# An attention and quantised-linear kernel: the tile work of two units done in every second unit

## The reference

```python
xn = _layernorm(x, axis=-1)
q = (xn @ Wq.T).reshape(n, s, HEADS, HEAD_DIM)              # k, v: 8 heads, each used twice
energy = jnp.einsum('nqhd,nkhd->nhqk', q, k) + _alibi_bias(s, s)
attn = jax.nn.softmax(energy / jnp.sqrt(jnp.float32(HEAD_DIM)), axis=-1)
out = jnp.einsum('nhqk,nkhd->nqhd', attn, v).reshape(n, s, HEADS * HEAD_DIM) @ Wo.T + bo

x_scale = jnp.maximum(jnp.max(jnp.abs(xn), -1, keepdims=True), 1e-6) / 127.0
x_q = jnp.clip(jnp.round(xn / x_scale), -128, 127).astype(jnp.int8)
lin = (x_q @ weight_q.T) * x_scale * weight_scale[None, :] + bias

x + out + lin
```

## Time and profile before

| | us |
|---|---|
| median of 3 runs | 1603.3 (1603.0 to 1604.26) |
| the profiled execution | 1604.17 |
| its span on the core | 1602.4 |
| TensorE busy | 1567.9, 98% |
| VectorE busy | 1429.5, 89% |
| ScalarE busy | 1220.8, 76% |
| GpSimd busy | 1066.9, 67% |

### The profile page before, as it was taken

The page is one execution under the profiler, slowest core; times in us unless marked ns, Lnnn a source line. Parts: engine busy times, 40 slices in busy tenths (PEclk is TensorE's granted clock), DMA queues, the critical chain, the costliest instruction groups (busy, mean ns, idle before and its releaser), DMA issues.

```text
span 1602.4 us, 53471 instructions
## 1 busy us (share of the span) xinstructions
PE 1567.9 (98%) x22012; PEld 785.0 (49%) x22012; DVE 1429.5 (89%) x1666; ACT 1220.8 (76%) x2394; POOL 1066.9 (67%) x1595
## 2 busy tenths in 40 slices
PE   5899999999999999999999999999999999999998
PEld 4344444545545545545545545545545545444443
DVE  6999999999999999999999999999999998999981
ACT  4477777777787787787787787787787787888875
POOL 5577787787777777777777777777777776333332
PEclk9999999999999999999999999999999999999999
DMA  8222222232232232223233223223223222111111
GB/s 195 71 69 59 72 75 62 77 79 79 81 79 80 82 78 80 82 75 83 81 77 81 82 73 85 82 75 83 81 73 85 79 67 62 52 52 50 45 46 54
DMA packets 182215, 121.03 MB, mean 76 GB/s; under 512 B 99988, under 2 KB 154644, under 8 KB 181972
## 3 DMA queue, kind: packets, MB, share of 16 engines
q1 hardware_dynamic: 181972, 117.62, 27.4%
HBM read 81.40 MB, written 35.63 MB: 73 GB/s over the span
## 4 chain that ended last, share of the span: by engine, by line
PE 83%; DVE 7%; SPq 4%; issue 3%; DMA 2%; POOL 1%; ACT 1%; DVEq 0%; POOLq 0%; ACTq 0%
PE ps_pv L1227 25%; PE ps_ring L1163 24%; PE ps_row L1163 24%; DVE row_max L885 4%; PE ps_ring L1259 3%; SPq L417 3%; PE ps_ring L1278 3%; DMA token_b<-token_dram 2%; PE ps_ring L1262 1%; PE ps_ring L1272 1%; DVE xn L812 1%; PE ps_row L1251 1%; DVE stats L802 1%; ACT probs L1048 1%; PE ps_ring L1178 0%
## 5 line engine op out<-in xcount | busy, mean ns | idle before, releaser
L885 DVE TENSOR_REDUCE row_max<-ps_row 128x1 f32<-128x1024 f32 x1024 | 1204.5, 1215 | 109.4 <-PE ps_row L1163 108.5
L1048 ACT ACTIVATE probs<-ps_ring 128x512 f32<-128x512 f32 x2048 | 1114.0, 600 | 216.1 <-PE ps_ring L1163 165.2
L1163 PE MATMUL ps_ring<-q,k 122*32 122x512 bf16 x8192 | 727.9, 379 | 1.7 <-ACT probs L1048 1.0
L1163 PE MATMUL ps_row<-k,q 120*32 120x512 bf16 x8192 | 635.7, 380 | 10.8 <-issue 4.9
L674 POOL TENSOR_TENSOR probs<-probs,near 128x256 f32<-128x256 f32 x512 | 380.8, 744 | 301.9 <-ACT probs L1048 255.9
L1227 PE MATMUL ps_pv<-probs,v_unit 128*32 128x512 f32 x4096 | 537.4, 593 | 5.5 <-POOL probs L674 5.5
L1163 PEld LDWEIGHTS ps_row<-k,q 120*32 120x32 bf16 x8192 | 240.4, 97 | 327.1 <-issue 159.5
L1163 PEld LDWEIGHTS ps_ring<-q,k 122*32 122x32 bf16 x8192 | 232.3, 95 | 318.4 <-issue 129.4
L1227 PEld LDWEIGHTS ps_pv<-probs,v_unit 128*32 128x32 f32 x4096 | 130.9, 110 | 81.6 <-POOL probs L674 10.9
L697 POOL TENSOR_TENSOR xt_step<-xt,token_b 128x256 f32<-128x256 f32 x53 | 45.8, 863 | 66.2 <-PE ps_ring L1163 46.0
L1259 PEld LDWEIGHTS ps_ring<-xn_t,wqk 128*128 128x128 f32 x636 | 78.7, 192 | 2.4
(11 more groups left out here) (85 smaller groups left out, 916.2 us busy)
## 6 DMA issues: line engine op xcount, KB each, us to landing
parts_dram<-parts SPq DMA_DIRECT2D x59, 288.0 KB, 3.3
token_b<-token_dram SPq DMA_DIRECT2D x53, 256.0 KB, 3.4
q<-parts_dram SPq DMA_DIRECT2D x128, 96.0 KB
q<-parts_dram SPq DMA_DIRECT2D x128, 64.0 KB
att_dram<-att_unit SPq DMA_DIRECT2D x126, 64.0 KB
att_t<-att_dram SPq DMA_DIRECT2D x56, 128.0 KB, 2.9
out<-out_tile SPq DMA_DIRECT2D x55, 128.0 KB, 2.9
xt<-x_t SPq DMA_DIRECT2D x53, 128.0 KB, 3.1
```

Source lines behind the costliest of these rows:

```text
L885: dve.tensor_reduce(row_max[:, par, e, qb:qb + 1], ps_row[qb % 2][:, :], AX_X, ALU.max, negate=True).then_inc(row_max_found, 1)
L1048: act.activation(probs[:, c % PBUFS, e, h * HALF:(h + 1) * HALF], ring_bank(u, c, e, h), ACT.Exp, scale=SCALE).then_inc(ring_freed, 1)
L1163: mm = pe.matmul(to[at, :], weights[:, at], moving, start=start, stop=stop)
```

## The change

Tiles are worked on in pairs. TensorE makes and projects two tiles in every odd unit and none in even ones (`made_unit`, `projected_unit`): in odd u, tiles u+9 and u+10 are made and tiles u-9 and u-8 projected, with `outputs` of both first and then `qkv_whole` of both, in four items of the ring. VectorE normalises two tiles and finds the statistics of two in odd units, at the same place of c=1, and none in even ones. GpSimd goes on turning one tile a unit; xt, xn_t and xq_t have four buffers (xt had four already), the scales eight. Of a pair, GpSimd splits the first tile at c=1 and the second at c=2 and c=3, weighs the first's linear result at c=4 and adds it at c=7, the second's at c=1 and c=2 of the next unit. Scaling, rounding and keeping a turned tile stand at c=4, 5 and 6. The first tiles' linear results are weighed at c=1 and added at c=4 of even units. Token factors are stored in pairs and loaded one a unit, ahead of `place_max` and no longer behind `load_set`. x is loaded two units earlier. At the start, quantised tiles are turned one step later. At the end, tile 55 is projected in unit 63 with tile 54, and the first part of the last sequence's projection goes over units 62 and 63, four products each.

```diff
-X_AHEAD = PREP_AHEAD + 3
+X_AHEAD = PREP_AHEAD + 5
+PAIR = 2
+TURNED = 4
-SCALES = 4
+SCALES = 8
+def made_unit(t):
+
+    return t - PREP_AHEAD + 1 + (t + 1) % PAIR
+
+
+def projected_unit(t):
+    return t + OUT_BEHIND - t % PAIR
 def flags_of(u):
 
+    pairs = u % PAIR == 1
-        made=0 < u and u - 1 + PREP_AHEAD < TILES,
-        normed=u + 1 + PREP_AHEAD < TILES,
-        stats=u + 2 + PREP_AHEAD < TILES,
+        made=[t for t in range(PREP_AHEAD, TILES) if made_unit(t) == u],
+        normed=[PREP_AHEAD + 1] * (u == 0) + [t for t in (u + PREP_AHEAD + 1, u + PREP_AHEAD + 2)
+                                             if pairs and t < TILES],
+        stats=([PREP_AHEAD + 2, PREP_AHEAD + 3] * (u == 0)
+               + [t for t in (u + PREP_AHEAD + 3, u + PREP_AHEAD + 4) if pairs and t < TILES]),
...
-        proj=u >= OUT_BEHIND,
+        proj=[t for t in range(TILES) if projected_unit(t) == u],
...
-        xn_t = sb("xn_t", [P, 2, EC, P])
-        xq_t = sb("xq_t", [P, 2, EC, P], BF16)
+        xn_t = sb("xn_t", [P, TURNED, EC, P])
+        xq_t = sb("xq_t", [P, TURNED, EC, P], BF16)
...
@@ sp: unit @@
-                if f["normed"]:
-                    store_token(u + 1 + PREP_AHEAD)
-                if f["made"]:
-                    store_parts(u - 1 + PREP_AHEAD, (u - 1 + PREP_AHEAD) % 2)
+                for t in f["normed"]:
+                    store_token(t)
+                for t in f["made"]:
+                    store_parts(t, t % 2)
...
+                if f["token"]:
+                    load_token(u + 1 + PREP_AHEAD)
                 if not f["last"]:
                     place_max(u + 1, (u + 1) % SETS)
...
-                if f["normed"]:
-                    load_token(u + 1 + PREP_AHEAD)
...
@@ gpsimd: unit @@
+                    if c == 1:
+                        for made in f["made"][:1]:
+                            split_high(made)
+                            split_middle(made)
+                    if c == 2:
+                        for made in f["made"][1:]:
+                            split_high(made)
...
+                    if c == 3:
+                        for made in f["made"][1:]:
+                            split_middle(made)
...
+                    if f["prev"] and c in (1, 2):
+                        for made in flags_of(u - 1)["made"][1:]:
+                            if c == 1:
+                                weigh_linear(made)
+                            else:
+                                add_weighted(made)
...
@@ vector: unit @@
-                    if c == 1 and f["normed"]:
-                        normalise(t + 1, (t + 1) % 2)
-                        find_largest(t + 1, (t + 1) % 2)
-                        find_scale(t + 1, (t + 1) % 2)
-                    if c == 1 and f["stats"]:
-                        wait(dve, x_loaded, 16 * (t + 2 - X_AHEAD + 1))
-                        find_stats(t + 2, t % 2)
+                    if c == 1:
+                        for t in f["normed"]:
+                            normalise(t, t % 2)
+                            find_largest(t, t % 2)
+                            find_scale(t, t % 2)
+                        for t in f["stats"]:
+                            wait(dve, x_loaded, 16 * (t - X_AHEAD + 1))
+                            find_stats(t, t % 2)
...
@@ tensor: unit @@
                     if c == 1:
-                        if f["made"] or f["proj"]:
-                            outputs(u, f)
-                        if f["made"]:
-                            qkv_whole(u)
+                        for t in f["proj"] or f["made"]:
+                            outputs(u, f, t % PAIR)
+                        for t in f["made"]:
+                            qkv_whole(u, t)
```

More of the change, by code:

```diff
@@ L109, in ring_places @@
             if c == 1:
-                items += [(u, "outputs")] * (f["made"] or f["proj"])
-                items += [(u, "qkv")] * f["made"]
+                items += [(u, "outputs", t % PAIR) for t in f["proj"] or f["made"]]
+                items += [(u, "qkv", t % PAIR) for t in f["made"]]
             if c == 5 and not f["last"]:
@@ L287, in build @@
         xt_loaded = [sem(f"xt_loaded{i}") for i in range(2)]
-        token_stored = sem("token_stored")
+        token_stored = [sem(f"token_stored{i}") for i in range(2)]
         token_loaded = [sem(f"token_loaded{i}") for i in range(2)]
@@ L340, in build @@
         CONSTS = 16 * 4
+        FIRST_BOTH = min(t for t in range(PREP_AHEAD, TILES) if flags_of(made_unit(t))["proj"])
         ALIBI = 16
@@ L354, in wait_lin_kept, with stored_tokens, finished @@
         def wait_lin_kept(eng, t):
-            u = t - PREP_AHEAD + 1
+            u = made_unit(t)
             if flags_of(u)["proj"]:
-                eng.wait_ge(lin_scaled, u - OUT_BEHIND + 1)
+                eng.wait_ge(lin_scaled, t - FIRST_BOTH + 1)
             else:
-                wait_freed(eng, u, "outputs")
+                wait_freed(eng, u, "outputs", t % PAIR)
+        def stored_tokens(t):
+            return 16 * ((t - PREP_AHEAD) // 2 + 1)
+        def finished(u):
+            return [t for t in range(TILES - BLOCKS)
+                    if u == min(projected_unit(t) + t % PAIR, UNITS - 1)]
         def run_units(unit):
@@ L750, in finish @@
             def finish(t):
-                wait_freed(pool, t + OUT_BEHIND, "outputs")
+                wait_freed(pool, projected_unit(t), "outputs", t % PAIR)
                 if t < PREP_AHEAD:
@@ L782, in unit @@
                         gather_v(u + 1, (u + 1) % 2)
-                    if c == 6 and f["stats"]:
-                        find_rstd(t + 2, t % 2)
+                    if c == 6:
+                        for later in f["factor"]:
+                            find_rstd(later, later % 2)
                     if c == 6 and f["turned"]:
                         keep_rounded(t)
-                    if c == 6 and u < PREP_AHEAD:
-                        add_first_linear(u)
-                    if c == 7 and f["proj"]:
-                        finish(u - OUT_BEHIND)
+                    if c == 7:
+                        for made in f["made"][:1]:
+                            add_weighted(made)
+                    if f["prev"] and c in (1, 2):
+                        for made in flags_of(u - 1)["made"][1:]:
+                            if c == 1:
+                                weigh_linear(made)
+                            else:
+                                add_weighted(made)
+                    if c == 1:
+                        for first in f["first_linear"]:
+                            weigh_first_linear(first)
+                    if c == 4:
+                        for first in f["first_linear"]:
+                            add_first_linear(first)
+                    if c == 7:
+                        for done in finished(u):
+                            finish(done)
             run_units(unit)
@@ L1252, in project_last, with qkv_whole @@
                           start=(c == 0 and i % 2 == 0), stop=False)
-            def qkv_whole(u):
-                t, bank = u + PREP_AHEAD - 1, take_bank(u, "qkv")
+            def qkv_whole(u, t):
+                bank = take_bank(u, "qkv", t % PAIR)
                 pe.wait_ge(xn_t_ready, t + 1)
```

196 lines of the change are left out of this document (93 added, 103 removed).

## The result

The changed kernel takes 1619.96 us (median of 4 runs, 1619.15 to 1620.67), against 1603.15 for the kernel before on the same chip (4 runs, 1601.17 to 1604.26): the ratio is 1.0106, with 1.0089 to 1.0124 as its 95% interval. It is slower by 16.8 us. 1626 was forecast, with 1608 to 1640 as the range. The profiled execution took 1620.67, its span 1618.9.

A forecast was written before the change was run, and what follows sets the result against it. TensorE was taken as the bound, with VectorE's side work just hidden (0.11 us in hand). Terms 0.9 + 0.6 - 0.6 + 20.8 + 3.1 - 2.5 + 0.4 = +22.7 on 1604.17 gave 1626 as median; range 1608 to 1640.

The forecast's parts named there:

- Odd units: Units carrying two tiles on TensorE: 2 x 2.88 + 0.21 = 5.97 of tile work, so 26.86 us a unit, no wait.
- 0.86 in hand: VectorE's slack at c=1 of odd units: 0.11 + 2.88 of cover - 2.13 of added tile work.
- Even units: Without tile work as cover, TensorE waits 0.85 to 1.37 us for VectorE at i=6; 1.3 taken, 22.19 a unit.
- Units 9 to 53: Middle of the kernel: 23 odd units and 22 even ones, 1106.0 against 1085.2 us, so +20.8.
- Units 1 to 8: Units that don't project: 192.8 against 193.4 us, so -0.6, with waits of 3.00 in unit 1 and 1.10 in odd ones.
- Start and unit 0: Start: last quantised tile turned a step later, +0.9; unit 0: one more tile's statistics at c=1, +0.6.
- Units 54 to 61, 62 and 63: End of the kernel: units that only project +3.1, unit 62 -2.5 with projections moved out, unit 63 +0.4.
- The earlier load takes that away: Token factors loaded ahead of the maxima: removes GpSimd's three-microsecond late start on the turned tile, gains nothing.
- TensorE alone as the bound: Rival: VectorE's wait in even units stays small, the change is faster, 1587 without any wait; chance 0.10.
- GpSimd always first: Rival: GpSimd's 0.74 us falls on the norm in nearly all even units, wait 1.6, 1635 us; chance 0.15.
- A wait on SP in odd units: Rival: second tile's parts late, maxima placed late, TensorE waits at even units' start; 1640 and more; chance 0.10.
- GpSimd clear of the norm: Rival: no GpSimd operation beside the norm, wait 0.85 in even units everywhere, 12.5 less, 1613 us; chance 0.10.

The follow-up runs named there:

- extra_odd6: Changed kernel with six more VectorE reductions of 256 values at c=1 of odd units 11 to 53, results unused: 1637.6 us, ratio 1.0219.
- linear_later: Changed kernel with GpSimd's second-tile weighing at c=2, its adding at c=3 and first tiles' weighing at c=3 in even units: 1615.37 us, ratio 1.0073.
- token_late: Changed kernel with the token factors loaded behind the set again, as in the kernel before: 1627.27 us, ratio 1.0148.
- before_token: Kernel before with only the token factors' load moved ahead of the maxima, as the change has it: 1597.33 us, ratio 0.9965.
- mid_sp: Changed kernel, even units: norm between reductions i=6 and i=7, turn back between i=8 and i=9, maxima ahead of attention on SP: 1584.46 us, ratio 0.9883.
- spread34: Changed kernel with the reciprocals and norm at c=3 and the turn back at c=4 of even units, SP's order unchanged: 1604.46 us, ratio 1.0018.
- before_mid: Kernel before, every unit: norm between reductions i=6 and i=7, turn back between i=8 and i=9, maxima ahead of attention on SP: 1599.12 us, ratio 0.9975.
- s45_sp: Changed kernel, even units: norm at c=4, turn back at c=5, maxima ahead of the attention's store and load on SP: 1594.76 us, ratio 0.9949.

## Why the prediction was right, and where its steps were not

**Odd units: right.** 26.86 was forecast and is what all 23 odd units from 9 to 53 show to 0.02. That the ring holds when a tile follows a tile is shown by the 0.45 at the change of tiles. "0.86 in hand" was half of what extra_odd6 shows, 1.68. The term that failed is the tile work of 2.13: it contained an xn of 0.82 that had GpSimd beside it, and without it is 1.72; 0.11 + 0.41 + 2.88 - 1.72 = 1.68. It cost the forecast nothing, since slack isn't time.

**Even units: right mechanism, size within its bounds.** "It waits 0.85", with 1.37 as the other end and 1.3 taken. Measured were 22.07 - 20.89 = 1.18 in the middle, and 0.97 without contention (linear_later). The 0.12 by which 0.85 is low is the turn back, which now follows the norm that it depends on: 0.46 from start to start (1437.10 to 1437.56 in unit 56), where xn, which doesn't, follows at 827.58 - 827.24 = 0.34. What the norm loses beside GpSimd is 0.21, between the forecast's 0 and 0.52; taking half was a choice between two readings, and it came out near. By the rule of the Trainium skill ("SBUF - State Buffer", the section on two separate sides: the first of the two keeps the shared port for its whole instruction) 1635 was given, with 0.74 more: GpSimd had in fact begun first, 0.38 earlier, and the norm did end 0.29 behind it, at 805.80 after 804.79 + 0.72 = 805.51. So the trace agrees with the rule, and the rival priced the whole operation where only what is left of it at the norm's start counts. Units 4, 6 and 8 show the rival nearly whole: there the weighing of a first tile began 0.06 before the norm, the norm took 0.95, and the units take 22.40, a wait of 1.51 where that rival had 1.6.

**Units 9 to 53**: +20.8 forecast, +18.1 measured, and 22 x (1.3 - 1.18) = 2.6 is the difference.

**Units 1 to 8: wrong size**, -0.6 against -3.4. Unit 1's wait was put at 3.00; the bracket shows 1.82, and by the period it is 25.13 - 20.89 - 2.11 = 2.13. The odd units' 1.10 is 25.25 - 20.89 - 4.01 = 0.35. Both used the 2.13 of tile work, which holds for a late load of the token factors: token_late, which has that, has -0.1 in these units, and of its unit 1 all but the fall of the clock is the forecast's 26.0.

**Start and unit 0**: +1.5 forecast, +0.85 measured. Unit 0's wait rose from 1.27 to 1.80, as forecast (0.5 against 0.6). The start's 0.9 was about 0.3 in the two profiled executions: the first ring matmul of unit 0 stands at 70.02 against 69.70. As the start differs by over 1 us between executions, 0.9 is neither borne out nor refuted.

**Units 54 to 61, 62 and 63**: +3.1, -2.5, +0.4 forecast; +2.6, -2.2, +0.5 measured.

**"The earlier load takes that away, but GpSimd isn't the bound, so nothing is gained": this step failed.** The load is worth some 6 us (before_token, token_late). GpSimd isn't the bound, but it sits beside VectorE's run, and VectorE had 0.11 in hand in unit 30. Nor is the start three microseconds late: GpSimd was at work until 795.43 and idle for 1.66, and in before_token it starts 1.70 earlier against the turn of pv. Unit 30 was also no typical unit for the norm, 0.43 where the median of all units is 0.64. That the sum was still near has a reason: every row that it was added up from had the late load, and the change with the load left late costs 23.7, where 22.7 was forecast. By stretch, token_late has +22.2 in units 9 to 53 (20.8 forecast) and -0.1 in units 1 to 8 (-0.6). So the term that was put at nothing is about the size of the gap between 1626 and 1620. Some of the nearness is luck, since token_late's sum holds 1.7 of a fallen clock that nobody had reckoned with.

**Rivals.** TensorE alone as the bound (1587, turning point at a wait of 0.57): fell, the wait is twice that; mid_sp shows what that kernel would be, 1584. GpSimd always first: it is first in the even units from 4 to 52, at the prices above, and not from unit 54 on. A wait on SP in odd units: fell for this change; it is what came in spread34, when the store of the attention was late. GpSimd clear of the norm (1613): fell; linear_later, which makes it so, takes 1615.4.

**Still open.** Why unit 11 takes 24.31 in the kernel before, before_token and before_mid (units 9 and 10 have the wait of pv shown above), and which part of mid_sp's lead over before_mid is due to GpSimd's moved additions and which to the earlier load. Other places for the norm in odd units weren't tried.

## What to carry to other kernels

When an engine runs in order through two buffers, what hides its side work is not its mean load but the cover that stands at that very place: ask of each burst what the other engine does meanwhile, and when a change gathers the cover in half of the units, spread the other halves' bursts into the small idle gaps that the consumer has anyway (here 0.24 us of each two blocks). Move with it everything that its queue holds up. And a load that an idle engine waits for isn't free: it decides beside whom that engine then works.

## What the hardware showed that was not expected

- TensorE's granted clock fell to 0.77 and 0.80 in the two stretches of 4 us around a wait of 2.58 us (the experiment with tile work in every unit), and row blocks took 1.7 times as long (1.04 against 0.61). It fell in eleven of 21 such units; in the same run unit 30, with a wait of 2.57, kept 23.66 and the full clock, and so did units 14 and 16 with waits of 3.0 (24.09 and 24.08). Waits of 1.2 us in every even unit of the changed kernel left the unit at 22.07 throughout. What tells the two kinds of unit apart isn't known from these runs.
- The norm's end behind GpSimd's is nearly a constant: 0.29 us in the earlier trace rows, in unit 30 of the changed kernel (805.51, 805.80), in s45_sp (848.17, 848.46) and in token_late (810.00, 810.29), while its duration was 0.95, 0.63, 0.68 and 1.05. It holds in every one of the 39 norms of the kernel before that took more than 0.45, with 0.28 to 0.29. So what such a norm costs is read from where GpSimd's operation ends, not from how long that operation is.
- Behind the norm VectorE started the instruction that needs its result 0.12 us later than one that doesn't (0.46 against 0.34), so a short independent instruction between them costs less than its own time.
